# Attention stage of a gated cross-attention kernel: values products put directly behind score pairs, output projection in two halves

## The reference

```python
x, lat = _ln(ctx), _ln(x)                # 120 context rows, 256 own rows, per batch
q = lat @ w_q                            # 8 heads of 64
k, v = split(concat([x, lat]) @ w_kv)    # 376 keys
sim = einsum('bhid,bhjd->bhij', q, k) * 64 ** -0.5      # masked
attn = softmax(sim, axis=-1)
out = einsum('bhij,bhjd->bhid', attn, v)
x1 = x + gate * _ln(out @ w_out)
```

## Time and profile before

| what | value |
|---|---|
| time, median of three runs | 2256.03 us |
| span of the profiled execution | 2253.4 us |
| TensorE matmul busy | 2227.8 us, 99% of the span |
| VectorE, ScalarE, GpSimd busy | 79%, 57%, 30% |
| VectorE and ScalarE in the first 17 of 40 slices | mostly 8 and 7 tenths |
| mean granted TensorE clock | 1.000 of full |
| first stage (batches 0 to 31) | about the first 1121 us |

### The profile page before, as it was taken

How to read it: one execution, slowest core, us unless ns; L and a number is a source line. 1 busy time by engine, 2 the same in 40 slices (tenths; PEclk the granted TensorE clock), 3 DMA queues, 4 the chain that set the end, 5 groups by cost and what they waited for, 6 DMA issues and landing times. The chain is left out here.

```text
span 2253.4 us, 48207 instructions
## 1 busy us (share of the span) xinstructions
PE 2227.8 (99%) x15396; PEld 1877.8 (83%) x15396; DVE 1771.8 (79%) x6078; ACT 1284.9 (57%) x3250; POOL 668.4 (30%) x1162
## 2 busy tenths in 40 slices
PE   8999999999999999999999999999899999999998
PEld 5777777777777777777799999999788888888887
DVE  5888888888888888888775555555599999999997
ACT  6776777677777777776544333433354554555553
POOL 1123233233233232232220000001355555555542
PEclk9999999999999999999999999999999999999999
DMA  6221010010110010110052222222221121222210
GB/s 235 73 95 31 27 40 30 29 39 29 31 38 27 32 39 27 33 32 27 15 155 85 85 72 80 85 66 69 63 60 60 60 62 54 63 64 64 63 43 19
DMA packets 111641, 129.55 MB, mean 57 GB/s; under 512 B 14898, under 2 KB 98089, under 8 KB 111264
## 3 DMA queue, kind: packets, MB, share of 16 engines
q1 hardware_dynamic: 98249, 105.06, 14.4%
q0 software_dynamic: 12288, 21.21, 3.3%
q10 hardware_dynamic: 855, 0.19, 0.0%
HBM read 84.26 MB, written 54.53 MB: 62 GB/s over the span
## 5 line engine op out<-in xcount | busy, mean ns | idle before, releaser
L715 ACT ACTIVATE a_prob<-a_prob,a_nmax 128x376 f32<-128x376 f32 x512 | 307.0, 604 | 3.4 <-DVE a_nmax L861 3.2
L1440 ACT ACTIVATE e_hidden<-e_first,keep_b 128x256 f32<-128x256 f32 x320 | 134.3, 472 | 282.5 <-PE e_first L80 279.5
L1132 PEld LDWEIGHTS a_turned<-keep_ident,a_prob 128*128 128x128 f32 x1518 | 174.2, 139 | 121.3 <-issue 103.6
L861 DVE CUSTOM_DVE_ANT_0 a_prob<-a_score,a_mask_row 128x376 f32<-128x376 f32 x512 | 262.9, 542 | 13.9 <-DVE r_lg L263 6.2
L1132 PE MATMUL a_turned<-keep_ident,a_prob 128*128 128x128 f32 x1518 | 260.5, 280 | 2.2 <-ACT a_probT L723 1.2
L723 ACT ACTIVATE a_probT<-a_turned 128x384 f32<-128x384 f32 x256 | 125.9, 492 | 221.2 <-PE a_turned L1132 216.1
L80 PE MATMUL e_second<-e_w,e_hidden 128*128 128x256 f32 x1920 | 239.6, 284 | 0.0
L80 PEld LDWEIGHTS e_second<-e_w,e_hidden 128*128 128x128 f32 x1920 | 232.6, 192 | 0.0
L177 POOL TENSOR_SCALAR r_var<-r_mv 128x2 f32<-128x2 f32 x64 | 12.3, 192 | 673.1 <-issue 600.0
L873 DVE TENSOR_SCALAR a_prob<-a_prob,a_rden 128x376 f32<-128x376 f32 x512 | 206.9, 431 | 2.2
L880 DVE COPY a_probT<-a_turned 128x384 f32<-128x384 f32 x250 | 139.2, 557 | 82.6 <-PE a_turned L1132 78.4
(11 more groups left out here) (223 smaller groups left out, 5165.3 us busy)
## 6 DMA issues: line engine op xcount, KB each, us to landing
w_in<-W SPq DMA_DIRECT2D x32, 512.0 KB, 4.0
slots<-a_zeros SPq DMA_DIRECT2D x8, 1280.0 KB, 8.9
keep_rows<-slots SPq DMA_DIRECT2D x40, 256.0 KB, 3.9
answers<-e_y SPq DMA_DIRECT2D x40, 256.0 KB, 2.2
a_xn<-x SPq DMA_DIRECT2D x32, 256.0 KB, 2.9
a_xr<-x SPq DMA_DIRECT2D x32, 256.0 KB, 2.9
x<-r_x SPq DMA_DIRECT2D x32, 256.0 KB, 3.2
w_in<-x SPq DMA_DIRECT2D x32, 256.0 KB, 2.7
```

The source lines that it names most:

```text
L715: nc.scalar.activation(prob[:, u % 4, a], prob[:, u % 4, a], ACT.Exp, bias=nmax[:, u % 4, a:a + 1], scale=-1.0, accum_out=den[:, u % 4, a: ...
L861: nc.vector.tensor_tensor_reduce(prob[:, u % 4, a], score[SCORE_AT[u][a]][:, 0:NKV], mask_row[:, p], -1.0, 3.0e38, ALU.add, ALU.min, nmax[ ...
L1132: last = nc.tensor.transpose(turned_keys(b, u, a)[0:hi - lo, j], prob[:, u % 4, a, lo:hi], ident[:])
L1440: nc.scalar.activation(hidden[:, 2 * j + i], first[:, j, i * CH:(i + 1) * CH], ACT.Relu, bias=b1[:, 2 * j + i, bass.ds(e, 1)]).then_inc(re ...
```

## The change

It only moves pieces; no engine gets another instruction of another size. `output` is called in two halves. TensorE's step becomes: S45, T3, t01, v0, t10, O first half, t11, O second half, count, t20, S67, T0, t21, q1, t30, k0, t31, q0, t40, k1, t41, S01, T1, t50, v2, t51, router turn, k2, t60, logits, t61, S23, T2, t70, turn_x, v1, t71, turn_c, k3, t00. The lists of ScalarE and VectorE are laid out anew to fit. T3 and t01 move from the end of a step to the next one.

```diff
-            def output(b):
+            def output(b, i):
+                if i == 0:
...
-                for i in range(QT):
-                    for k in range(KI):
...
+                for k in range(KI):
...
+                if i == QT - 1:
+                    last.then_inc(out_ok, 1)
...
                     scores(s - 2, p, 4)
                     scores(s - 2, p, 5)
+                if live(s - 3):
+                    times_v(s - 3, q, 3)
+                if live(s - 2):
+                    turn_prob(s - 2, 0, 1)
+                    project_v(s - 2, p, 0)
                     turn_prob(s - 2, 1, 0)
-                    project_v(s - 2, p, 0)
+                if live(s - 3):
+                    output(s - 3, 0)
+                if live(s - 2):
                     turn_prob(s - 2, 1, 1)
                 if live(s - 3):
-                    output(s - 3)
-                if live(s - 2):
-                    turn_prob(s - 2, 2, 0)
+                    output(s - 3, 1)
...
```

More of the change, by code:

```diff
@@ L762, in step @@
                 if live(s - 2):
-                    att_high(s - 2, 0)
-                    turned_out(s - 2, 3, 0)
-                    exps(s - 2, 6, 1)
+                    exps(s - 2, 7, 1)
                 if live(s - 1):
-                    q_high(s - 1, q, 1)
+                    q_high(s - 1, q, 0)
+                if live(s - 2):
+                    turned_out(s - 2, 4, 0)
+                if live(s - 1):
+                    k_high(s - 1, q, 1)
+                if here(s - 3):
+                    x1_standardise(eng, s - 3, q)
+                if live(s - 1):
+                    exps(s - 1, 0, 0)
+                    exps(s - 1, 0, 1)
+                if live(s - 2):
+                    att_high(s - 2, 1)
+                    turned_out(s - 2, 5, 0)
+                if live(s - 1):
+                    exps(s - 1, 1, 0)
+                if isinstance(s, int) and s == B + 1:
+                    w1_higher(0)
+                    w1_higher(1)
+                if live(s - 1):
+                    v_out(s - 1, q, 2)
+                if here(s - 3):
+                    router_in(eng, s - 3)
+                if live(s - 1):
+                    exps(s - 1, 1, 1)
+                if live(s - 2):
+                    turned_out(s - 2, 6, 0)
+                if live(s - 1):
+                    k_high(s - 1, q, 2)
                 if live(s):
@@ L772, in step @@
                     nc.scalar.activation(wkv[:, 0, :, INNER:], stage_kv[:, :, INNER:], ACT.Copy).then_inc(w_high, 1)
-                if live(s - 2):
-                    turned_out(s - 2, 4, 0)
                 if live(s - 1):
[L776 to L803, removed]
+                    exps(s - 1, 2, 0)
+                    exps(s - 1, 2, 1)
                 if live(s - 2):
@@ L931, in step @@
                     weights_lower(3, wo[:], stage_o)
+                if live(s - 2):
+                    row_max(s - 2, p, 4, 0)
                 if live(s - 1):
@@ L962, in step @@
                 if live(s - 2):
+                    normalise(s - 2, 2, 1)
+                    row_max(s - 2, p, 6, 0)
+                if live(s - 1) and not (isinstance(s, int) and s == 1):
+                    kvin_low(s - 1, q, 1)
+                if live(s - 2):
+                    normalise(s - 2, 3, 0)
+                    over_sum(s - 2, 4)
                     turned_out(s - 2, 2, 1)
-                    normalise(s - 2, 3, 0)
+                    row_max(s - 2, p, 6, 1)
+                    normalise(s - 2, 3, 1)
+                    att_low(s - 2, 0)
                 if here(s - 3):
@@ L1018, in step @@
                     row_max(s - 1, q, 2, 0)
+                    row_max(s - 1, q, 2, 1)
+                    over_sum(s - 1, 0)
+                if here(s - 3):
+                    logits_shift(eng, s - 3)
+                if live(s - 1):
+                    normalise(s - 1, 0, 0)
+                    row_max(s - 1, q, 3, 0)
                 if live(s - 2):
@@ L1237, in step @@
                     turn_prob(s - 2, 6, 0)
+                if here(s - 3):
+                    router_logits(eng, s - 3)
+                if live(s - 2):
+                    turn_prob(s - 2, 6, 1)
                 if live(s - 1):
```

140 lines of the change are left out of this document (61 added, 79 removed).

## The result

The changed kernel is slower by 0.24%: 2261.71 us (median of 11 runs, 2260.25 to 2262.88) against 2255.94 us (2255.19 to 2258.79, 11 runs) of the kernel before on the same chip. The ratio is 1.0024, with a 95% interval of 1.0015 to 1.0032. The forecast was 2250 us and faster. The profiled execution has a span of 2259.8 us, 6.4 more than before.

The account below looks back on a forecast made before the run. TensorE alone was taken to set the first stage's step: 0.60 us saved less 0.40 us of waits gives 0.20 a step, 6 us over 30 steps, from 2256.0 to 2250 us; range 2236 to 2262.

Parts of the forecast that it names:

- TensorE's own sum: TensorE's pieces in one first-stage step, before any waits, would take about 0.60 us less.
- The joint: Scores directly followed by a values product on TensorE: costs 0.15 us, between 0 and 0.30.
- Rival A: In first-stage steps, the joint is free or no turn waits: 2236.5 us; chance 0.22.
- rival B: On TensorE, the joint costs 0.30 us, dearer than one change of the array's division: 2263.5 us; chance 0.13.
- Where waits stand: Turns t31 and t41 wait for ScalarE's copy; other places lose nothing or 0.05 us.
- The chain: From t10 through VectorE's row_max and ScalarE's exponentials and copies: t31 can start 10.29 us after t10, t41 13.57.
- The size of the waits: Waits at t31 and t41 lose 0.3 us a step, taken as 0.4 with margins for hand-overs.
- rival C: One more wait in the step, candidate t51, takes the 0.20 us gain: no change, 2256 us; chance 0.15.
- The ends of the stage: Step 2 and steps 33 and 34: waits and fillers rule before and after; nothing put, 3 us either way.
- Step period: One first-stage step takes 33.9 us, 34.09 before; the prediction is wrong under 33.6 or over 34.1.

Follow-up runs that it names:

- act + tail: The changed kernel with both edits, ScalarE's exponentials behind the copies and step 33's weight copies back at their earlier places: 2245.97 us.
- two more moves: act + tail with counts_in ahead of out_stat on VectorE and the copy of unit 6 ahead of exps(1, 1) on ScalarE: 2243.74 us.
- act: The changed kernel with exps(6, 1) and exps(7, 1) moved behind the copies of turned units 3 and 4 on ScalarE: 2247.32 us.
- pad: The changed kernel with one unread VectorE copy of 128 x 256 numbers added ahead of row_max(6, 1): 2268.35 us.
- tail: The changed kernel with step 33's w1_higher behind the copy of unit 6 and w1_lower behind logits_shift on VectorE: 2257.84 us.
- joints undone: act + tail with turns t01, t50 and t70 put back between scores and values product, the fourth joint kept: 2260.66 us.

## Why the prediction was wrong

**TensorE's own sum: right in the difference.** Without the lengthening that waits bring (listed below), a step of the changed kernel takes 34.22 - 0.76 = 33.46 us in the mean of steps 4 to 30; forecast 34.09 - 0.60 = 33.49. act + tail, with most of the waits gone, has 33.69. The lengths of single turns were too low: the sixteen take 5.70 before and 5.17 after without waits, where 5.37 and 4.88 were put, because a turn ahead of the count, the router's pieces or turn_x takes 0.33 to 0.38 (t70, behind T2, takes 0.38 and not the 0.30 of the forecast). Both sums are off by the same, so their difference holds.

**The joint: right.** 0.15 was taken, between 0 and 0.30. S and T start 1.464 apart at three of the joints (1.545 at the fourth, where T0 waits, and 1.464 there too in the kernel with two more moves), and each joint is worth 0.17 when it is undone. Rival A's free joint would have shown 1.37, rival B's dear one up to 1.62. By the rule of the Trainium skill, TensorEngine Tiling (Array Packing), section Tiling Modes, Key Properties (a change of the mode drains TensorE), the joint had to be paid. The trace agrees: 1.464 and not the 1.37 of a free joint. It adds that a joint is paid once, where a turn in between pays 0.17 more.

**Where waits stand: right for t31 and t41, incomplete for the rest.** act removes these two waits by moving nothing but ScalarE's exponentials, and pad lengthens the one at t31 by the whole 0.20. The chain was the named one.

**The size of the waits: the first step that failed.** A step loses 0.40 us to waits, the prediction said. It loses 0.76, by the mean length of each piece in steps 4 to 30 against the same piece without a wait:

| piece | after | without a wait | lost |
|---|---|---|---|
| k0, behind it t31 | 1.37 | 1.11 | 0.26 |
| k1, behind it t41 | 1.30 | 1.11 | 0.19 |
| t31, t41 themselves | 0.275, 0.449 | 0.245, 0.42 | 0.06 |
| S67, behind it T0 | 1.545 | 1.464 | 0.08 |
| t20, t61 | 0.456, 0.449 | 0.42 | 0.07 |
| turn_c | 0.186 | 0.133 | 0.05 |
| logits, t71 | 0.835, 0.349 | 0.813, 0.325 | 0.05 |

The first three rows are 0.51, where 0.40 was put; in act these four pieces are 0.50 shorter, and the step 0.49. What the trace shows as longer is the chain's first link: row_max(5, 0) starts 0.71 behind t10, and I had taken the 0.53 of a copy. With 0.18 more the 0.2 to 0.3 of the working becomes 0.4 to 0.5. And a turn that waited takes 0.03 more itself, which no row of before had shown. The other four rows are 0.25. For T0 and t61 the working had a slack of 0.1 us and of none (needed at 5.5, ready at 5.4; 1.14 against 1.15) and put nothing or hardly anything; t20, turn_c, the logits and t71 were not worked out at all. Each such place cost 0.02 to 0.08. Not all of the 0.25 is shown to be waits of this order, though. turn_c takes 0.186 in this profile alone; with the same lists in tail and in pad it takes 0.138 and 0.134. t20 behind the count takes 0.448 to 0.458 in every changed kernel, and t71 0.34 to 0.36, whatever else was moved, so there the neighbour may be what lengthens them. The whole saving was to be 0.20; the 0.36 more turned it into a loss of 0.12 to 0.13 a step. That is rival C's mechanism, another wait that takes the gain, though in no way at t51, where C had put it.

**The ends of the stage: the second step that failed.** "I put nothing, with 3 us either way." They cost 3.7 us (0.3 at the start, 3.4 in the last steps). w1_higher, two long activations that run in step 33 only, had come to stand ahead of router_in, and TensorE, whose order is fixed, waited for it. tail shows it: 2.7 us of the 3.4 go with this one move. Behind the wait TensorE's clock fell in this execution, which is some 1.5 of the 2.7; it need not (pad, and the three runs of the change at a mean granted clock of 1.000, which take 2260.3 us). The Trainium skill, TensorE: Matmul & The Clock Gate, in Part 1, gives nearly twice the spacing of 128-wide bf16 matmuls for the lower clock (107 ns against 56). Here the eight fillers took 1.82 us where act + tail, at the same place and full clock, has 0.97, so the trace agrees in the ratio.

**Step period.** The prediction called itself wrong over 34.1; measured 34.22. The sign was wrong. That the time, 2261.7, lies near B's 2263.5 and just inside the upper end of the range is luck: B's dear joint is not there, and C, whose mechanism is, was given 15% and 2256 us.

Open: why a row_max that waits for a turn starts 0.71 behind it, when copies that waited for one started 0.53 behind it before and 0.58 in this same step (614.10 to 614.68); no run isolated it. Where the remaining 0.6 us of the tail come from is open too, beyond the 0.36 us wait at the logits. The start of the stage (S45 of step 3) lay between 62.67 and 66.73 us in the profiled executions of the changed orders. That goes with the clock and not with the edits. It lay at 62.67 to 63.33 where the granted clock stayed at 1.00 up to there (the change, act, joints undone). It lay at 63.96 to 64.81 with one stretch at half clock, near 38 to 41 us. In tail, with two such stretches (0.66 from 12 to 17 us, 0.57 from 40 to 44), it lay at 66.73, and in pad, with a longer one (0.57 from 37 to 45), at 66.50. So a difference of single spans below 4 us says little.

## What to carry to other kernels

Where a change of order saves less than the slack it uses up, the sum is won or lost in the waits, and "just in time" by hundredths of a microsecond should not be priced at nothing: here such places cost 0.02 to 0.08 each. Give the copy that releases the bottleneck the first place in its engine's list, ahead of work that has slack (here the exponentials: 14 us for two moved lines), and look at a wait through the distance of starts, since a pipelined TensorE shows little idle time for it, or none. Look at the steps in which one-off work is slipped in as closely as at the loop: one wait of 1.4 us in step 33 cost 2.7 us more than one of 0.4 where the clock fell behind it, and 1.1 more by itself.

## What was unexpected of the hardware

- Of a wait of about 0.27 us ahead of a turn the trace shows next to nothing: k0 at 1.38 instead of 1.11 has its modelled end 0.11 before the turn and no bracket, k0 at 1.57 shows 0.30 (of 0.46).
- A turn that waited takes 0.03 us more to the next start: 0.275 instead of 0.245 between two full pieces, and 0.449 instead of 0.42 ahead of scores.
- From a turn to the next one that waits for VectorE's copy, with only the count between them: 1.23 us.
- After 1.42 us of idle time in a stretch already thinned by waits, the granted clock was 0.76 over 7 us in the change, but 1.00 in pad; after 0.36 us in the same place it stayed at 1.00 in all five profiled executions. Where it fell, the tail was some 1.5 us longer.
